# Expert weights fetched tile by tile, and the last stage's weight quantised after the experts, in a two-layer transformer kernel

## The reference, cut to what matters

```python
x = x + L0_xattn(layernorm(x), ctx_768)      # 16 heads of 16
x = x + L0_ffn(layernorm(x))                 # below
x = x + L1_xattn(layernorm(x), ctx_768)      # 8 heads of 64
x = x + L1_ffn(layernorm(x))                 # MX-quantised linear

def L0_ffn(x):
    x = x + causal_attention(ln1(x))
    nx2 = ln2(x)
    vals, idx = top_k(nx2 @ gate_W, 2)       # 8 experts, 2 a row
    for e in range(8):
        h = gelu(nx2 @ fc1_w[e].T + fc1_b[e])          # 256 -> 1024
        moe += gates[..., e] * (h @ fc2_w[e].T + fc2_b[e])   # 1024 -> 256
    return x + moe

def L1_ffn(x):                               # FP6 grid, one scale per 32 numbers
    return dequantised(x) @ dequantised(weight).T + bias     # weight 256 x 256
```

## Time and profile before

| | |
|---|---|
| runs | median 1996.81 us, 1996.51 to 1998.34 |
| the profiled execution | 1994.65 us, its span 1992.7 us |
| TensorE (PE) busy | 1882.7 us, 94% |
| TensorE's weight loads (PEld) | 1647.4 us, 83% |
| VectorE (DVE) | 1575.0 us, 79% |
| ScalarE (ACT) | 1264.5 us, 63% |
| GpSimd (POOL) | 1097.2 us, 55% |
| moved by DMA | 124.38 MB, mean 62 GB/s |

### The profile page before, as it was taken

How to read it: one execution, slowest core, us unless ns; L and a number is a source line. 1 busy time by engine, 2 the same in 40 slices (tenths; PEclk the granted TensorE clock), 3 DMA queues, 4 the chain that set the end, 5 groups by cost and what they waited for, 6 DMA issues and landing times.

```text
span 1992.7 us, 61725 instructions
## 1 busy us (share of the span) xinstructions
PE 1882.7 (94%) x20887; PEld 1647.4 (83%) x20887; DVE 1575.0 (79%) x3452; ACT 1264.5 (63%) x2719; POOL 1097.2 (55%) x1680
## 2 busy tenths in 40 slices
PE   7999999999799999779999999959999999999996
PEld 5888888887578878579999999958888888888885
DVE  6788878887268888678888888847888888888886
ACT  2555555555367777547777777747777777776773
POOL 4565566554257676623333333377776777676751
PEclk9999999999899999889999999979999999999998
DMA  8223322330081111211111111141111111111100
GB/s 233 89 86 94 107 86 87 114 107 14 30 297 32 37 37 39 66 56 39 37 37 37 39 39 37 34 134 57 42 33 39 34 39 34 39 34 39 34 15 10
DMA packets 101539, 124.38 MB, mean 62 GB/s; under 512 B 9874, under 2 KB 93586, under 8 KB 101010
## 3 DMA queue, kind: packets, MB, share of 16 engines
q1 hardware_dynamic: 95330, 108.83, 17.7%
q0 software_dynamic: 6144, 14.69, 2.5%
HBM read 70.01 MB, written 53.48 MB: 62 GB/s over the span
## 4 chain that ended last, share of the span: by engine, by line
PE 52%; DVE 3%; issue 1%; ACT 1%; POOL 0%; DMA 0%; ACTq 0%; DVEq 0%; POOLq 0%; SPq 0%
PE ps_quad L1425 11%; PE ps_out L1444 9%; PE ps_quad L181 6%; PE ps_quad L101 4%; PE ps_out L113 4%; PE ps_turned L107 4%; PE ps_quad L1858 3%; PE ps_proj L1878 3%; PE ps_turned L181 3%; PE ps_proj L181 2%; PE ps_proj L1883 1%; PE ps_proj L1432 1%; DVE c_negmax L118 1%; ACT c_probs L133 0%; PE ps_quad L1873 0%
## 5 line engine op out<-in xcount | busy, mean ns | idle before, releaser
L1341 POOL TENSOR_TENSOR e_w2L<-w,e_w2H 128x1024 fp32r<-128x1024 f32 x63 | 149.4, 2372 | 307.0 <-ACT e_w2H L1312 307.0
L1425 PE MATMUL ps_quad<-e_xT,e_w_now 128*128 128x128 f32 x2016 | 242.3, 279 | 11.7 <-DVE e_xT L1379 11.7
L1425 PEld LDWEIGHTS ps_quad<-e_xT,e_w_now 128*128 128x128 f32 x2016 | 234.0, 194 | 13.8 <-issue 8.1
L363 ACT ACTIVATE a_probsT<-ps_quad 125x1792 f32<-125x1792 f32 x96 | 159.8, 1665 | 101.5 <-PE ps_quad L532 101.5
L1320 ACT ACTIVATE e_act_T<-ps_quad,fc_b 128x128 f32<-128x128 f32 x504 | 136.8, 382 | 115.9 <-PE ps_quad L1425 114.1
L133 ACT ACTIVATE c_probs<-ps_quad,c_negmax 112x375 f32<-112x375 f32 x256 | 143.6, 570 | 66.5 <-DVE c_negmax L118 66.5
L1392 DVE TENSOR_TENSOR e_aL<-e_act_T,e_aH 128x1024 fp32r<-128x1024 f32 x63 | 152.5, 2421 | 35.7 <-ACT e_aH L1327 35.7
L1444 PE MATMUL ps_out<-e_w2H,e_aH 128*128 128x256 f32 x504 | 148.4, 294 | 9.6 <-issue 5.0
L125 DVE TENSOR_SCALAR c_probs<-c_probs,c_recip 112x375 f32<-112x375 f32 x256 | 150.8, 630 | 4.5
L420 DVE TENSOR_REDUCE a_negmax<-ps_turned 112x2 f32<-112x750 f32 x128 | 120.1, 939 | 34.0 <-PE ps_turned L518 33.8
L118 DVE TENSOR_REDUCE c_negmax<-ps_quad 112x2 f32<-112x750 f32 x128 | 114.1, 932 | 40.9 <-PE ps_quad L101 40.4
(11 more groups left out here) (353 smaller groups left out, 6022.1 us busy)
## 6 DMA issues: line engine op xcount, KB each, us to landing
slots<-a_zeros SPq DMA_DIRECT2D x60, 512.0 KB, 4.9
a_cT<-in_ctx_t SPq DMA_DIRECT2D x32, 375.0 KB, 3.4
c_cT<-in_ctx_t SPq DMA_DIRECT2D x32, 375.0 KB, 3.2
w<-in_fc_t SPq DMA_DIRECT2D x2, 4096.0 KB, 19.1
w<-in_fc_t SPq DMA_DIRECT2D x8, 1024.0 KB, 12.2
e_xg<-slots SPq DMA_DIRECT2D x63, 128.0 KB, 2.0
slots<-e_y SPq DMA_DIRECT2D x63, 128.0 KB, 1.7
out<-c_fo SPq DMA_DIRECT2D x32, 112.0 KB, 1.9
```

The source lines that it names most:

```text
L363: act.activation(probsT[:, 2 * i:2 * i + 2, :, :].rearrange("p c r x -> p r c x"), quad[0:KC, :, 0:2 * HALF].rearrange("p r (c x) -> p r c ...
L1341: pool.tensor_tensor(w2L[:, 0:HALF], weights_half(e, 0), w2H[:, 0:HALF], ALU.subtract).then_inc(w2_low, 1)
L1425: last = pe.matmul(hidden[par][:, c // 4, (c % 4) * TILE:(c % 4 + 1) * TILE], w1_now[:, k, c * 128:(c + 1) * 128], xT[par][:, k, :], start ...
```

## The change

It has three parts, and some moves that come with them.

1. *First weights.* The buffer for all experts' `w1` becomes two buffers for one expert each. At the start of self-attention SP loads expert 0's alone. In the experts SP fetches the 1 MB of tile t + 2's expert into the buffer of tile t, once TensorE has made tile t's first product (`first_weights`). TensorE reads the buffer directly and waits for the fetch; the copy to `w1_now` is gone from VectorE. The rows of a tile are fetched two tiles ahead too. An unused tensor, `room`, keeps the other addresses where they were.
2. *The last stage's weight* is quantised in one piece, with ops of 512 columns: three of them at the last tile, ten behind its output `y`. TensorE turns it at the start of its list for the last stage, and the copy out of PSUM is ScalarE's.
3. *The loads for the last stage* go out at tile 1, and ScalarE rounds `wk` and `wv` behind its work on tile 1. GpSimd copies the first row numbers ahead of its wait for the last store.

GpSimd takes the same low halves as before. The lines of the changed kernel stand some 5 to 16 further down: `xT` is L1386 there, `y` L1394, `aL` L1399, `w2L` L1401, the fetch of first weights L1288, `c_ratio` L1761.

```diff
                 sp.wait_ge(values_mm, 1)
-                for half in range(2):
-                    sp.dma_start(mem["w1"][:, 4 * half:4 * half + 4, :, :], w["fc1_t"].rearrange("e (k p) f -> p e k f", p=128)[:, 4 * half:4 * half + 4])\
-                      .then_inc(mem["w1_in"], 16)
+                sp.dma_start(mem["w1"][:, 0:1, :, :], mem["w1_rows"][:, 0:1, :, :]).then_inc(mem["w1_in"][0], 16)
                 for e in range(NE - 1):
...
@@ experts @@
-        w1_now = sb("w1_now", [128, 2, HID])[:, :, :]
-        wf, mx = sb("wf", [128, 2 * D]), {n: sb(f"mx_{n}", [128, D]) for n in ("t", "magic", "q", "d")}
+        wf, mx = sb("wf", [128, 2 * D]), {n: sb(f"mx_{n}", [128, 2 * D]) for n in ("t", "magic", "q", "d")}
...
@@ experts, sync @@
+                def rows_in(t, par):
+                    at = first_row(t)
+                    wait(sp, xT_mm, t - 1)
+                    sp.dma_start(xg[par], slots[bass.ds(at, TILE), :]).then_inc(x_in[par], 16)
+
+                def first_weights(t, par):
+                    e = sp.value_load(mem["tile_expert"][0:1, bass.ds(t, 1)], min_val=0, max_val=NE - 1)
+                    wait(sp, h_mm, t - 1)
+                    sp.dma_start(mem["w1"][:, par:par + 1, :, :], mem["w1_rows"][:, bass.ds(e, 1), :, :]).then_inc(mem["w1_in"][par], 16)
+
                 def step(t, par):
...
+                    ahead = t + 2
                     if isinstance(t, int) and t == -1:
-                        sp.wait_ge(mem["routed"], 1)
+                        rows_in(0, 0)
+                        rows_in(1, 1)
+                        first_weights(1, 1)
...
+                    elif exists(ahead, MOE_TILES):
+                        rows_in(ahead, par)
                     if exists(t - 2, MOE_TILES):
                         at = first_row(t - 2)
                         sp.wait_ge(y_ready, t - 1)
                         sp.dma_start(slots[bass.ds(at, TILE), :], y[par]).then_inc(y_out[par], 16)
-                    if isinstance(t, int) and t == MOE_TILES - 1:
-                        sp.wait_ge(w1_ready, MOE_TILES)
+                    if exists(t, MOE_TILES) and exists(ahead, MOE_TILES):
+                        first_weights(ahead, par)
+                    if isinstance(t, int) and t == 1:
                         mem["preload"](sp)
...
@@ experts, scalar @@
                         weights_high(e, 1)
+                    if isinstance(t, int) and t == 1:
+                        mem["round_weights"](act)
...
@@ experts, vector @@
-                def quantise_half(k):
-                    part = wf[:, k * D:(k + 1) * D]
-                    for action in quantise_steps(dve, link, part, part, mx, D // MX, 128):
...
+                quantise = quantise_steps(dve, link, wf, wf, mx, 2 * D // MX, 128)
+                EARLY = 3
...
-                        wait(dve, mem["w1_in"], 32)
-                        wait(dve, h_mm, nxt)
-                        dve.tensor_copy(w1_now, mem["w1"][:, bass.ds(e, 1), :, :].rearrange("p a k f -> p (a k) f")).then_inc(w1_ready, 1)
+                        wait(dve, h_mm, nxt - 1)
                         dve.wait_ge(xT_mm, nxt + 1)
...
-                    if isinstance(t, int) and t in (0, 1):
+                    if isinstance(t, int) and t == MOE_TILES - 1:
                         dve.wait_ge(bias_in, 32)
-                        quantise_half(t)
-                    if isinstance(t, int) and t == MOE_TILES - 1:
-                        dve.wait_ge(w_mm, 1)
-                        dve.tensor_copy(mem["wf_t"][:, :, :], wf_ps).then_inc(w_out, 1)
+                        for action in quantise[:EARLY]:
+                            action()
+                    if isinstance(t, int) and t == MOE_TILES:
+                        for action in quantise[EARLY:]:
+                            last = action()
+                        last.then_inc(w_ready, 1)
...
@@ experts, tensor @@
-                    if isinstance(t, int) and t == MOE_TILES - 1:
-                        pe.wait_ge(w_ready, 1)
-                        for i in range(2):
-                            for o in range(2):
-                                last = pe.transpose(wf_ps[:, i, o * 128:(o + 1) * 128], wf[:, o * D + i * 128:o * D + (i + 1) * 128], ident[:, :])
-                        last.then_inc(w_mm, 1)
                     if exists(t, MOE_TILES):
                         pe.wait_ge(xT_ready, t + 1)
-                        pe.wait_ge(w1_ready, t + 1)
+                        pe.wait_ge(mem["w1_in"][par], 8 * (t - par + 2))
...
@@ cross_last @@
+        def round_weights(act):
+            act.wait_ge(wk_in, 16)
+            act.activation(wkH[:, :, :], wk[:, :, :], ACT.Copy).then_inc(w_high, 1)
+            act.wait_ge(wv_in, 16)
+            act.activation(wvH[:, :, :], wv[:, :, :], ACT.Copy).then_inc(w_high, 1)
...
@@ cross_last, gpsimd @@
                 pool.wait_ge(v_split, 2)
+                index_rows(0, 0)
                 for i, tiles in enumerate(((MOE_TILES + 1) // 2, MOE_TILES // 2)):
                     pool.wait_ge(mem["y_out"][i], 16 * tiles)
                 fetch(0, 0)
...
@@ cross_last, scalar @@
+                    if isinstance(b, int) and b == -2:
+                        act.wait_ge(w_mm, 1)
+                        act.activation(mem["wf_t"][:, :, :], wf_ps, ACT.Copy).then_inc(w_out, 1)
...
@@ cross_last, tensor @@
-                pe.wait_ge(mem["w_out"], 1)
+                pe.wait_ge(mem["last_y"], MOE_TILES)
+                pe.wait_ge(mem["wf_ready"], 1)
+                for i in range(2):
+                    for o in range(2):
+                        last = pe.transpose(wf_ps[:, i, o * 128:(o + 1) * 128], mem["wf"][:, o * D + i * 128:o * D + (i + 1) * 128], ident[:, :])
+                last.then_inc(w_mm, 1)
                 pe.wait_ge(k_split, 2)
...
@@ program @@
-            for name, shape in (("w1", [128, NE, 2, HID]), ("w2", [128, NE, HID // 128, D])):
+            for name, shape in (("room", [128, ROOM]), ("w1", [128, 2, 2, HID]), ("w2", [128, NE, HID // 128, D])):
```

More of the change, by code:

```diff
@@ L40 @@
 MX_MAX = 7.5
+ROOM = 6 * 2 * HID
 def wait(eng, sem, value):
@@ L1297, in step @@
                         sp.dma_start(slots[bass.ds(at, TILE), :], y[par]).then_inc(y_out[par], 16)
-                    if isinstance(t, int) and t == MOE_TILES - 1:
-                        sp.wait_ge(w1_ready, MOE_TILES)
+                    if exists(t, MOE_TILES) and exists(ahead, MOE_TILES):
+                        first_weights(ahead, par)
+                    if isinstance(t, int) and t == 1:
                         mem["preload"](sp)
-                over_tiles(sp, step, 2)
+                step(-1, 1)
+                step(0, 0)
+                step(1, 1)
+                with sp.Fori(1, (MOE_TILES - 3) // 2) as i:
+                    step(2 * i, 0)
+                    step(2 * i + 1, 1)
+                for t in range(MOE_TILES - 3, MOE_TILES + 2):
+                    step(t, t % 2)
             @block.scalar
@@ L1424, in step @@
                             for k in range(2):
-                                last = pe.matmul(hidden[par][:, c // 4, (c % 4) * TILE:(c % 4 + 1) * TILE], w1_now[:, k, c * 128:(c + 1) * 128],
+                                last = pe.matmul(hidden[par][:, c // 4, (c % 4) * TILE:(c % 4 + 1) * TILE],
+                                                 mem["w1"][:, par, k, c * 128:(c + 1) * 128],
                                                  xT[par][:, k, :], start=(k == 0), stop=(k == 1))
@@ L1544, in _, with index_rows @@
             def _(pool):
-                def fetch(b, par):
-                    wait(pool, mixed, 2 * (b - 1))
+                def index_rows(b, par):
                     for s in range(TOP):
@@ L1549, in fetch @@
                     last.then_inc(indexed, 1)
+                def fetch(b, par):
+                    if not (isinstance(b, int) and b == 0):
+                        wait(pool, mixed, 2 * (b - 1))
+                        index_rows(b, par)
                     pool.wait_ge(indexed, b + 1)
@@ L2022, in step @@
                         wait(pe, o_ready, b - 1)
+                        if isinstance(b, int) and b == 1:
+                            pe.wait_ge(w_out, 1)
                         core.pe_values(pe, 0, v_of(1 - par))
```

36 lines of the change are left out of this document (11 added, 25 removed).

## The result

The changed kernel takes 1982.1 us (median of 5 runs, 1980.91 to 1985.12); before, 1996.51 us over the 5 runs beside it. The ratio is 0.9934, 95% interval [0.9923, 0.9945]: 14.4 us less, 12.0 forecast, range 1979.5 to 1991.5. The profiled execution took 1980.91 us, its span 1978.8.

A forecast was written before the change was run, and what follows sets the result against it. TensorE was taken to bound the experts, so gains were sought in its holes. Terms -5.3, -9.0, -0.4 and +2.7 sum to -12.0 us, off the 1996.81 us median: 1984.8 us, range 1979.5 to 1991.5.

The forecast's parts named there:

- The load, -5.3: Start of self-attention: loading 8 MB instead of 15 lets the first scatters land in the usual 2.6 us; gain 5.3 us.
- no scatter takes over 3 us: Self-attention near 580 us: a sign that would show the forecast right, every scatter landing within 3 us.
- The start, -9.0, bounds 5 and 11.1: Start of the experts: without quantisation at tiles 0 and 1, tile 4 starts earlier; gain 9.0 us, between 5 and 11.1.
- The 1.2 us for a falling clock: Start of the experts: deduction, half of 2.4 us, for a product running longer if the clock falls during TensorE's wait.
- The 0.9 us for the refill: Start of the experts: deduction for the scalar engine waiting on last-stage loads queued behind tile 3's weights.
- The copies, 0: Steady expert tiles: VectorE's 63 copies to `w1_now` lie beside TensorE's work, so removing their 77 us gains 0.
- Rival (e): Steady expert tiles: the copy was in the rhythm; a lighter VectorE removes 1.2% idle, some 5 us more; chance 0.05.
- Transposes, -0.4: End of the experts: four weight transposes leave TensorE's full part for the gap ahead of the last stage; gain 0.4 us.
- The end, +2.7, bounds 1.3 and 5.4: Behind the last tile: ten quantisation ops delay the gates 7.7 us against 5.05 slack; loss 2.7 us, between 1.3 and 5.4.
- 1.3 booked: Behind the last tile: 1.3 us added because VectorE's quantisation ops can be held beside GpSimd.
- The fetch, 0: Expert tiles: a 1 MB fetch, 4.8 us plus about 1, lands within the 10.27 us before TensorE needs it; cost 0.
- Its lower end, "1980": Whole kernel: the forecast's own best case, 11.1 at the start and 1.3 at the end, about 3.5 us better.

The follow-up runs named there:

- the control: The changed kernel run once more, with nothing altered, beside later versions on one chip; 1981.23 us, ratio 0.9923.
- e2_copy: The changed kernel with a 128x2048 copy of fixed data on VectorE put back ahead of each `xT`; 1984.53 us, ratio 0.994.
- e5_preload_late: The changed kernel with the last stage's loads and the rounding of `wk` and `wv` moved back to the last tile; 1983.05 us, ratio 0.9927.

## Why the prediction was right, step by step

*The load, -5.3.* Right: s0 to s5 is 5.30 us shorter, and putting the burst back brings 5.34. One sign failed, that no scatter takes over 3 us: the first took 3.8, with the load over, but nothing waited for it. In the first profile 1.34 us seem to be given back at the end of the stage (s5 to tile 0, 251.11), in the control none (249.82). That is the clock and not the change: the two profiles with 251 us, this one and e2_copy, are the two whose granted clock is 0.83 from 815 to 825 us; in all others of the table it is 1.00.

*The start, -9.0, bounds 5 and 11.1.* Right in cause and size. Tile 4 starts 40.00 us behind tile 0 before, 30.30 in the changed kernel's first profile (-9.7), 28.88 in the control (-11.1, the upper bound). The 1.2 us for a falling clock was paid in one and not in the other. The 0.9 us for the refill was never paid: with the late loads (e5_preload_late) tile 3 stands where the control has it.

*The copies, 0.* Wrong, by 2.7 us: this is the step that failed. The forecast took "beside TensorE's work" from shares of busy time and saw no wait; but `xT` ended 0.14 us ahead of the product that reads it. 0.095 us a pair times the 29 pairs from tile 4 to tile 62 is 2.7. Rival (e) had the right place with 5 us for it, and against it the argument that the second product waits for others: true of the second product, and beside the point for the first.

*Transposes, -0.4.* Part of the 3.1 us between the first products of tiles 4 and 62 (401.50 to 398.36 us); the other 2.7 is the rhythm.

*The end, +2.7, bounds 1.3 and 5.4.* Right in cause, measured +1.42. The ops of 512 columns took 0.69 us, as estimated. Two were held by GpSimd (1.44 and 1.37 us, some 1.7 too long together; 1.3 booked): each lies beside an op of GpSimd and ends 0.3 to 0.6 us behind it. What the forecast carried over and should not have is the gates' own time: 3.14 us before (1312.77 to 1315.91), when GpSimd held them, 1.27 now (1305.34 to 1306.61), when GpSimd is at its gathers. The gather adds nothing to the 1.42 us: it was issued 4.29 us behind the last output instead of 3.60, but landed in 3.8 us instead of 4.8, so its rows were there after 8.1 us, and the gates, done after 9.92, bound alone.

*The fetch, 0.* Right: 4.9 us against 10.3, no wait for a DMA from 875 us to the end of the tiles, and the edge lies between two and three MB a tile.

*The range.* Its lower end, "1980", is off in the forecast's own sum: 3.5 us under 1984.8 is 1981.3. The measured 1982.1 lies inside either way.

By the first profile the terms come to -5.3, -9.7, -3.1 and +1.4, 16.7 us instead of 12.0. Against that stand 0.8 up to s0, 1.3 ahead of tile 0, 0.2 in the last tile and 0.4 in the rest, where the change does nothing or little: 13.9 of the span. So the forecast came close in part by luck: in this profile the missed 2.7 us and the smaller loss at the end met a scatter of about their size.

The Trainium skill (SBUF — State Buffer, section Who interferes with whom) says that a VectorE op with two SBUF inputs is blocked while a GpSimd op reads SBUF. The last `w2L` agrees: 3.33 us beside GpSimd's pieces, 1.21 without them. One of the two ops held at the end, L1212 with 1.37 us, has a single input, so this sentence alone does not cover it. The page's warning about one-input ops and descriptors no run here shows: beside the first gather stand two-input ops (L1215, L1216), and it landed sooner than before.

## What to carry to other kernels

An engine that shows no wait can still set the pace: compare the end of what it hands over with the start of its reader, and look for instructions whose length differs between like tiles. When a wait goes, price again what ran behind it, since the ops there may have been held by a neighbour that is now elsewhere. Cut profiles at marks and compare stretch by stretch; with the same code before a mark, the spread there says how much of a difference in span means nothing, and the granted clock of the stretch often says where it comes from.
